# Graph attention on one core: one Q product moved between scores and contexts, split over the array's upper and lower rows

## The chip, the core and the metric

One NeuronCore of a Trainium2 chip runs the whole program. The metric is device time in microseconds (us) from start to end of one execution. Engines run side by side, each through its own queue in order: PE (TensorE, matmuls into PSUM), DVE (VectorE), ACT (ScalarE), POOL (GpSimd) and SP (SyncE, here the queue that issues the DMAs). They meet only at semaphores.

## What is computed

The reference, cut to what matters. `B` is 128 graphs of `S` = 128 nodes, hidden size 384, six heads of 64.

```python
q = heads(x @ Wq + bq);  k = heads(x @ Wk + bk);  v = heads(x @ Wv + bv)
scores = einsum('bhqd,bhkd->bhqk', q, k) / sqrt(64)
probs = softmax(scores + where(adj, 0, -9e15)[:, None], axis=-1)
ctx = einsum('bhqk,bhkd->bhqd', probs, v)          # heads side by side again
out = layernorm(x + ctx @ Wf + bf)                 # over the last axis, eps 1e-5
```

## The kernel before, in words

The 128 graphs go in 32 groups of four (`e` = 0 to 3 names the graph in its group; 512 tokens). Group g is handled by `step`, and parts of three groups share a step. On PE a step is, in this order: the scores of group g (`scores`, L413), three products of Q or K for group g+1 (`qk_product`, L456), the contexts of group g-1 (`ctx_product`, L429), the other three Q or K products of g+1, the output products of g-1 (`out_product`, L449), and the V products of g+1 (`v_product`, L475). All projections (`split_product`, L404 to L411) are made of triples of matmuls of a rounded and a rest part (`hi`, `lo`) in fp32r: nine matmuls for one product, 128 rows by 128 columns of the array, with 512 moving columns for Q and K and 384 for V and output.

Scores and contexts use parts of the array. A head has 64 channels, so a scores matmul reads 64 rows, and two heads go as a couple on the upper and lower 64 rows, into different PSUM banks. A context matmul fills 64 of the array's columns, and two heads go as a couple on the two halves of the columns. In the trace each of these fp32 matmuls is two records, so that a stretch of 24 has 48.

PSUM has eight banks. `scores_ps` is banks 0 to 5: the scores of a group fill all six, the graph e = 0 in banks 0 and 3, e = 1 in 0, 3, 1 and 4, e = 2 in 1, 4, 2 and 5, e = 3 in 2 and 5. The contexts and outputs of g-1 go into banks 0, 3, 1, 4 (`CTX_BANKS`) while group g's scores may still lie there, so `ctx_product` waits on the semaphore `max_found`: two graphs of g must have been read before e = 0 and 1, three before e = 2 and 3 (L440). `work_ps` is the other two banks, which the Q, K and V products use in turn.

DVE reads the scores bank in `mask_and_max` (L626): six passes for a graph (scale, mask, write to `probs`, row maximum), then `neg_max` (L639). The first graph starts when the scores of two are done. ACT exponentiates (`exps`, six activations for a graph), and between them copies the Q and K products out of `work_ps` with the bias (`copy_qk`, L836, semaphore `qk_copied`). DVE inverts the sums (`invert_sums`), POOL multiplies (`normalise_probs`), DVE turns 32x32 blocks (`turn_blocks`), and SP stores and reloads them to finish the transpose (`store_blocks`, `load_blocks`, landing in `pT`), which the contexts of the next step read. ACT rounds the contexts (`round_ctx`), DVE takes the rest (`split_ctx`), PE makes the outputs, DVE adds x and the bias (`add_residual`) and finds mean and variance (`find_stats`), and POOL normalises (`normalise_y`). POOL also adds the bias row to x (`add_bias`, `x_bias`) and turns the adjacency into a mask. The order on every engine is that in which its `step` is written out.

Of the kernel before, what the change touches and what calls it, by code (L numbers as in the profile page):

```python
# [17 lines left out]
ALU = mybir.AluOpType  # L18
ACT = mybir.ActivationFunctionType
# [5 lines left out]
P = 128  # L25
# [5 lines left out]
KC = HID // P  # L31
# [18 lines left out]
TURNS = GROUPS // TURN - 1  # L50

QK_JOBS = [("q", 0), ("k", 0), ("q", 1), ("k", 1), ("k", 2), ("q", 2)]
CTX_BANKS = (0, 3, 1, 4)
NJ = len(QK_JOBS)
HALF = NJ // 2

WARM_UPS = (10, 4)
DMA = 16
# [27 lines left out]
def attention_block(nc, x, adj, wq, bq, wk, bk, wv, bv, wf, bf, out):  # L86
    ctx = ExitStack()
    with ctx:
# [3 lines left out]
        def sem(name):  # L92
            return ctx.enter_context(nc.semaphore(name))
# [70 lines left out]
        def ctx_bank(e):  # L164
            bank = CTX_BANKS[e]
            return scores_ps[:, bank * BANK:(bank + 1) * BANK]

        bias_bank = scores_ps[:, 5 * BANK:5 * BANK + HID]

        def stats_slot(e, n):  # L170
# [78 lines left out]
        exp_done = sem("exp_done")  # L249
        v_copied = sem("v_copied")  # L250
        qk_copied = sem("qk_copied")

        masked_ready = sem("masked_ready")
        x_biased = sem("x_biased")
# [1 line left out]
        rstd_ready = sem("rstd_ready")  # L256
        y_ready = sem("y_ready")
        last_y_ready = sem("last_y_ready")

        def first_of(i, c):  # L260

            return (TURN * i + c) * GROUP
# [140 lines left out]
        def _(pe):  # L403
# [9 lines left out]
            def scores(i, c):  # L413

                g, n = TURN * i + c, first_of(i, c)
                past(pe, qk_copied, g, per=NJ)
# [12 lines left out]
            def ctx_product(i, c, e):  # L429

                g, n = TURN * i + c, first_of(i, c) + e
                past(pe, v_copied, n)
                if isinstance(n, int) and n in TURNED_HERE:
                    pe.wait_ge(pT_copied, 2 * (TURNED_HERE.index(n) + 1))
                else:
                    past(pe, pT_landed[e], g, per=BLOCKS * DMA)
                if isinstance(g, int) and g == LAST:
                    past(pe, y_added, n - GROUP)
                else:
                    past(pe, max_found, first_of(i, c) + GROUP + max(e, 1) - (e == 3))  # L440
# [15 lines left out]
            def qk_product(i, c, j):  # L456

                mat, m = QK_JOBS[j]
                g, n = TURN * i + c, first_of(i, c)
                if isinstance(g, int) and g == 0:  # L460
                    pe.wait_ge(w_split[mat], m + 1)
                past(pe, xT_split, n + GROUP - 1)
                if j < 2:
                    past(pe, v_copied, max(n - GROUP, 0) + 2 + j if isinstance(n, int) else n - GROUP + 2 + j)
                else:
                    past(pe, qk_copied, g * NJ + j - 2)
                split_product(work_ps[j % 2][:, :], lambda k: (
                    w_hi[mat][:, k, m * P:(m + 1) * P], w_lo[mat][:, k, m * P:(m + 1) * P],
                    xT_hi[:, c % TURN, k, :], xT_lo[:, c % TURN, k, :]), qk_done)

            def v_operands(c, e):
                return lambda k: (xT_hi[:, c % TURN, k, tokens(e)], xT_lo[:, c % TURN, k, tokens(e)],
# [2 lines left out]
            def v_product(i, c, e):  # L475


                g, n = TURN * i + c, first_of(i, c) + e
                past(pe, xT_split, n)
                if e >= 2:  # L480
                    past(pe, v_copied, n - 2)
                elif not isinstance(g, int) or g > 0:
                    past(pe, qk_copied, g * NJ + NJ - 2 + e)
                split_product(work_ps[e % 2][:, 0:HID], v_operands(c, e), v_done)

            def first_v():
# [105 lines left out]
        def _(dve):  # L592
# [33 lines left out]
            def mask_and_max(e, n):  # L626
# [5 lines left out]
                for h in range(HEADS):  # L632
# [6 lines left out]
                nc.vector.tensor_scalar(neg_max[:, e, :], row_max[:, e, :], -1.0, None, ALU.mult  # L639
                                        ).then_inc(max_negated, 1)  # L640

            def turn_blocks(i, c, e, n):
# [39 lines left out]
            def step(i, c):  # L682
# [3 lines left out]
                for e in range(3):  # L686
                    mask_and_max(e, n + e)
                invert_sums(0, n)
                mask_and_max(3, n + 3)
                if real(g + 2):  # L690
                    for e in (0, 1):
                        turn_x(i, c + 2, e)
                invert_sums(1, n + 1)
                if real(g + 2):
                    for e in (2, 3):
                        turn_x(i, c + 2, e)
                turn_blocks(i, c, 0, n)
# [3 lines left out]
                turn_blocks(i, c, 1, n + 1)  # L701
                invert_sums(2, n + 2)
# [3 lines left out]
                turn_blocks(i, c, 2, n + 2)  # L706
                if real(g - 1):
                    for e in (0, 1):
                        add_residual(i, c - 1, e, n - GROUP + e)
                    find_stats(0, n - GROUP)  # L710
                invert_sums(3, n + 3)
                if real(g - 1):
                    find_stats(1, n - GROUP + 1)
                    for e in (2, 3):
                        add_residual(i, c - 1, e, n - GROUP + e)
                turn_blocks(i, c, 3, n + 3)
                if real(g + 2):
                    for e in range(GROUP):
                        split_x(c, e, n + 2 * GROUP + e)
                if real(g - 1):  # L720
                    for e in (2, 3):
                        find_stats(e, n - GROUP + e)

            def ending():
                i, c, n = LAST // TURN, LAST % TURN, LAST * GROUP
# [70 lines left out]
        def _(act):  # L796
# [34 lines left out]
            def copy_v(c, e, n):  # L831
                past(act, v_done, n)
                past(act, ctx_done, n - RING)
                nc.scalar.copy(v_sb[:, c % TURN * GROUP + e, :], work_ps[e % 2][:, 0:HID]).then_inc(v_copied, 1)  # L834

            def copy_qk(i, c, j):  # L836

                mat, m = QK_JOBS[j]
# [7 lines left out]
            def step(i, c):  # L846

                g, n = TURN * i + c, first_of(i, c)
                exps(0, n, end=2)
                copy_qk(i, c + 1, 0)  # L850
                exps(0, n, first=2)
                copy_qk(i, c + 1, 1)
                exps(1, n + 1)
# [4 lines left out]
                exps(2, n + 2, end=2)  # L858
                copy_qk(i, c + 1, 3)
                exps(2, n + 2, first=2)  # L860
                copy_qk(i, c + 1, 4)
# [3 lines left out]
                exps(3, n + 3)  # L865
                copy_qk(i, c + 1, 5)
# [183 lines left out]
```

## Time and profile before

| what | value |
|---|---|
| median of 3 runs | 1013.79 us (1013.69 to 1014.57) |
| the profiled execution's own time | 1014.83 us |
| its span in the profile | 1013.0 us |
| PE busy | 1001.5 us, 99% of the span |
| DVE, POOL, ACT busy | 705.5, 629.8, 583.8 us |
| granted PE clock | 0.998 of full speed |
| chain that ended last | PE 95% |

The busy shares say which engine is full; the chain of work that ended last says whether it also sets the end. The steps repeat, so one step in the middle (its scores start at 516.31 us) stands for thirty. T below is the time since the start of a step's scores.

### The profile page before, as it was taken

The numbers are of one execution on the slowest core, as the hardware profiler recorded it, in microseconds if no ns is written. First come the engines' busy times: TensorE is split into PE (matmuls) and PEld (weight loads), VectorE is DVE, ScalarE is ACT, GpSimd is POOL, SyncE is SP. The second block draws the span as 40 slices with busy tenths as digits, with TensorE's granted clock in tenths as the row PEclk, the third lists the DMA queues.
The fourth block names the chain that finished last, engine by engine and source line by source line (L and its number), as shares of the span: only waits on it lengthen the run. The fifth ranks groups of instructions, "written<-read, shape, count | busy, mean of one in ns | idle before, by whom it ended". The sixth has DMA issues, their size and how long they took to land.

```text
span 1013.0 us, 26785 instructions
## 1 busy us (share of the span) xinstructions
PE 1001.5 (99%) x7156; PEld 901.5 (89%) x7156; DVE 705.5 (70%) x2829; ACT 583.8 (58%) x2121; POOL 629.8 (62%) x649
## 2 busy tenths in 40 slices
PE   9999999999999999999999999999999999999996
PEld 8888999888999889998899998899988999988986
DVE  4567766767667677667676676776676766767776
ACT  4665556664556655566645566554666455665552
POOL 2527755567665577555676655775556766557756
PEclk9999999999999999999999999999999999999999
DMA  7366676666766766766667667666676676675443
GB/s 207 81 182 182 185 191 189 174 185 174 197 170 181 187 168 175 195 169 182 181 174 196 168 184 187 163 180 187 171 189 177 176 191 176 181 183 157 150 150 130
DMA packets 339163, 178.06 MB, mean 176 GB/s; under 512 B 222529, under 2 KB 323009, under 8 KB 339137
## 3 DMA queue, kind: packets, MB, share of 16 engines
q1 hardware_dynamic: 337648, 176.77, 63.8%
q10 hardware_dynamic: 1488, 0.98, 0.3%
q8 instruction: 11, 0.18, 0.1%
q14 instruction: 16, 0.12, 0.0%
HBM read 102.96 MB, written 74.71 MB: 175 GB/s over the span
## 4 chain that ended last, share of the span: by engine, by line
PE 95%; ACT 2%; DVE 1%; DMA 1%; issue 0%; DVEq 0%; ACTq 0%
PE work_ps L408 20%; PE work_ps L409 19%; PE work_ps L410 19%; PE scores_ps L444 9%; PE scores_ps L425 9%; PE scores_ps L408 6%; PE scores_ps L409 6%; PE scores_ps L410 6%; ACT probs L825 1%; DMA y_sb<-in_L_gnn_Wq 1%; DVE stats L666 0%; DMA x_in<-in_x 0%; DVE probs L633 0%; ACT qT L843 0%; PE scores_ps L502 0%
## 5 line engine op out<-in xcount | busy, mean ns | idle before, releaser
L979 POOL TENSOR_TENSOR probs<-probs,inv_sum 128x768 f32<-128x768 f32 x128 | 188.5, 1473 | 332.4 <-DVE inv_sum L652 332.4
L825 ACT ACTIVATE probs<-probs,neg_max 128x128 f32<-128x128 f32 x768 | 298.9, 396 | 100.5 <-DVE neg_max L639 100.5
L633 DVE CUSTOM_DVE_ANT_0 probs<-scores_ps,mask_bias 128x128 f32<-128x128 f32 x768 | 172.0, 285 | 83.0 <-PE scores_ps L425 81.9
L974 POOL TENSOR_SCALAR y_sb<-y_sb,mean_var,rstd 128x384 f32<-128x384 f32 x120 | 198.8, 1656 | 21.5 <-POOL rstd L968 21.5
L834 ACT COPY v_sb<-work_ps 128x384 f32<-128x384 f32 x128 | 61.6, 481 | 215.4 <-PE work_ps L410 215.4
L825 ACT ACTIVATION_READ_ACCUMULATOR probs<-probs,neg_max 128x1 f32 x768 | 149.3, 194 | 0.0
L962 POOL TENSOR_TENSOR x_bias<-x_in,bias_row 128x384 f32<-128x384 f32 x128 | 127.6, 1019 | 9.0 <-DVE bias_row L788 9.0
L408 PE MATMUL scores_ps<-wf_hi,cT_hi 128*128 128x384 f32 x384 | 130.1, 339 | 0.0
L409 PE MATMUL scores_ps<-wf_lo,cT_hi 128*128 128x384 f32 x384 | 129.9, 338 | 0.0
L410 PE MATMUL scores_ps<-wf_hi,cT_lo 128*128 128x384 f32 x384 | 129.7, 338 | 0.0
L408 PE MATMUL work_ps<-wv_hi,xT_hi 128*128 128x384 f32 x381 | 128.1, 336 | 0.6 <-ACT qT L843 0.4
L410 PE MATMUL work_ps<-wv_hi,xT_lo 128*128 128x384 f32 x381 | 127.5, 335 | 0.0
L409 PE MATMUL work_ps<-wv_lo,xT_hi 128*128 128x384 f32 x381 | 127.4, 334 | 0.0
L645 DVE STREAM_TRANSPOSE p_turned<-probs 128x768 f32<-128x768 f32 x126 | 120.9, 960 | 5.3 <-DMA p_out<-p_turned 3.7
L408 PE MATMUL work_ps<-xT_hi,wq_hi 128*128 128x512 f32 x288 | 116.1, 403 | 0.1
L408 PE MATMUL work_ps<-xT_hi,wk_hi 128*128 128x512 f32 x288 | 115.8, 402 | 0.0
L409 PE MATMUL work_ps<-xT_lo,wq_hi 128*128 128x512 f32 x288 | 113.0, 392 | 0.0
L409 PE MATMUL work_ps<-xT_lo,wk_hi 128*128 128x512 f32 x288 | 112.5, 391 | 0.0
L410 PE MATMUL work_ps<-xT_hi,wq_lo 128*128 128x512 f32 x288 | 112.4, 390 | 0.0
L410 PE MATMUL work_ps<-xT_hi,wk_lo 128*128 128x512 f32 x288 | 112.1, 389 | 0.0
L843 ACT ACTIVATE kT<-work_ps,bk_col 128x512 f32<-128x512 f32 x96 | 65.2, 679 | 61.1 <-PE work_ps L410 61.1
L660 DVE TENSOR_TENSOR y_sb<-scores_ps,x_bias 128x384 f32<-128x384 f32 x120 | 65.4, 557 | 47.6 <-PE scores_ps L410 47.6
(78 smaller groups left out, 1886.9 us busy)
## 6 DMA issues: line engine op xcount, KB each, us to landing
p_out<-p_turned SPq DMA_DIRECT2D x126, 384.0 KB, 2.8
pT<-p_out SPq DMA_DIRECT2D x504, 96.0 KB, 2.3
x_in<-in_x SPq DMA_DIRECT2D x128, 192.0 KB, 3.0
x_blocks<-in_x SPq DMA_DIRECT2D x360, 64.0 KB, 2.4
out<-y_sb SPq DMA_DIRECT2D x120, 192.0 KB, 2.2
adj_u<-in_adj SPq DMA_DIRECT2D x32, 64.0 KB, 2.1
out<-xT SPq DMA_DIRECT2D x4, 192.0 KB, 1.9
out<-qT SPq DMA_DIRECT2D x4, 192.0 KB, 2.1
```

What stands on the lines that cost most here:

```text
L408: nc.tensor.matmul(dst, s_hi, m_hi, start=k == 0, stop=False)
L409: nc.tensor.matmul(dst, s_hi, m_lo, start=False, stop=False)
L410: last = nc.tensor.matmul(dst, s_lo, m_hi, start=False, stop=k == n_chunks - 1)
L425: last = nc.tensor.matmul(scores_ps[:, score_cols(e, h)], qT[rows, c, h // 2, tokens(e)], kT[rows, c, h // 2, tokens(e)], start=True, stop ...
L444: last = nc.tensor.matmul(dst[half:half + HEAD, h // 2 * SEQ:(h // 2 + 1) * SEQ], v_sb[:, c % TURN * GROUP + e, h * HEAD:(h + 1) * HEAD], ...
L633: last = nc.vector.tensor_tensor_reduce(out=probs[:, e, h, :], in0=scores_ps[:, score_cols(e, h)], in1=mask_bias[:, e, :], scale=SCALE, sc ...
L645: nc.vector.transpose(p_turned[:, e % 2, :, :, :].rearrange("p b h j -> p h b j"), probs[:, e, :, :].rearrange("p h (b k) -> p h b k", b=B ...
L660: nc.vector.tensor_tensor(y_slot(e, n), ctx_bank(e)[:, 0:HID], x_bias[:, c % TURN * GROUP + e, :], ALU.add).then_inc(y_added, 1)
L825: last = nc.scalar.activation(probs[:, e, h, :], probs[:, e, h, :], ACT.Exp, bias=neg_max[:, e, h:h + 1], scale=1.0, accum_out=row_sum[:, ...
L962: nc.gpsimd.tensor_tensor(x_bias[:, slot, :], x_in[:, slot, :], bias_row[:, :], ALU.add).then_inc(x_biased, 1)
L974: nc.gpsimd.tensor_scalar(y_slot(e, n), y_slot(e, n), mean_var[:, at, 0:1], rstd[:, at, 0:1], ALU.subtract, ALU.mult).then_inc(y_ready, 1)
L979: nc.gpsimd.tensor_tensor(probs[:, e, :, :], probs[:, e, :, :], inv_sum[:, e, :].unsqueeze(2).broadcast_to([P, HEADS, SEQ]), ALU.mult).the ...
```

## The change

One product of Q for group g+1, job j = 0, moves from the full array to couples: for each of the three 128-row chunks of the contraction, rows 0 to 63 go to one matmul and rows 64 to 127 to another, into banks 6 and 7 (`qk_halves`). That is 18 matmuls instead of nine, and the same number of columns for each. ACT copies the upper half with the bias (`copy_half`), and DVE adds the lower half to it (`sum_halves`, semaphore `qk_summed`). On PE this product stands alone between scores and contexts, and the five others follow the contexts. Jobs 1 and 2 wait for `qk_summed`. The first group's products are as before.

On DVE the addition stands behind `invert_sums(0)` and ahead of the fourth graph's `mask_and_max`; turning of blocks moves forward and `split_ctx`, `add_residual` and `find_stats` move back. On ACT the exponentials come more in one piece, and the copies of jobs 1 to 5 later. POOL and SP are unchanged.

```diff
+            def qk_halves(i, c, j):
+                mat, m = QK_JOBS[j]
+                n, cols = first_of(i, c), slice(m * P, (m + 1) * P)
+                past(pe, xT_split, n + GROUP - 1)
+                past(pe, v_copied, n - 1)
+                for k in range(KC):
+                    for w, moving in ((w_hi, xT_hi), (w_hi, xT_lo), (w_lo, xT_hi)):
+                        for half in range(2):
+                            rows = slice(half * HEAD, (half + 1) * HEAD)
+                            last = nc.tensor.matmul(half_bank(j, half), w[mat][rows, k, cols],
+                                                    moving[rows, c % TURN, k, :],
...
+                last.then_inc(qk_done, 1)
...
 def step(i, c):                                    (PE)
                 scores(i, c)
-                for j in range(HALF):
-                    qk_product(i, c + 1, j)
+                for j in range(HALVED):
+                    qk_halves(i, c + 1, j)
                 if real(g - 1):
                     for e in range(GROUP):
                         ctx_product(i, c - 1, e)
-                for j in range(HALF, NJ):
+                for j in range(HALVED, NJ):
                     qk_product(i, c + 1, j)
...
+                elif j < HALVED + 2:
+                    pe.wait_ge(qk_summed, HALVED * (g - 1) + 1)
...
+            def sum_halves(i, c, j):
+                dst = (qT if mat == "q" else kT)[:, c % TURN, m, :]
+                dve.wait_ge(half_copied, HALVED * (TURN * i + c - 1) + j + 1)
+                nc.vector.tensor_tensor(dst, half_bank(j, 1), dst, ALU.add).then_inc(qk_summed, 1)
...
+            def copy_half(i, c, j):
+                nc.scalar.activation(dst[:, c % TURN, m, :], half_bank(j, 0), ACT.Identity,
+                                     bias=col[:, m:m + 1], scale=1.0).then_inc(half_copied, 1)
```

PE of the kernel before, in a step, from the end of the scores (`scores_ps<-kT,qT`): the first of three products on the full array.

```order
L425 MATMUL scores_ps<-kT,qT 128x128 x23
L408 MATMUL work_ps<-xT_hi,wq_hi 128x512 [waits v_copied,xT_split]
L409 MATMUL work_ps<-xT_lo,wq_hi 128x512
L410 MATMUL work_ps<-xT_hi,wq_lo 128x512
L408 MATMUL work_ps<-xT_hi,wq_hi 128x512
```

PE of the changed kernel at the same place; L501 is the matmul of `qk_halves`, x2 a couple.

```order
L440 MATMUL scores_ps<-kT,qT 128x128 x23
L501 MATMUL work_ps<-xT_hi,wq_hi 128x512 [waits v_copied,xT_split]
L501 MATMUL work_ps<-xT_hi,wq_hi 128x512
L501 MATMUL work_ps<-xT_lo,wq_hi 128x512 x2
L501 MATMUL work_ps<-xT_hi,wq_lo 128x512 x2
L501 MATMUL work_ps<-xT_hi,wq_hi 128x512 x2
```

Before, 27 such matmuls stand between the scores and the contexts; now 18, as nine couples, and the contexts come right behind them.

DVE of the kernel before, in a step, from the last `neg_max` on: transposes of x, the block transposes `p_turned` and the rests of the contexts `cT_lo`.

```order
L639 TENSOR_SCALAR neg_max<-row_max 128x6 [waits max_found]
L617 STREAM_TRANSPOSE xT<-x_blocks 128x384 [waits xT_split,x_blocks_loaded1] x2
L652 RECIPROCAL inv_sum<-row_sum 128x6 [waits probs_ready,exp_done]
L617 STREAM_TRANSPOSE xT<-x_blocks 128x384 [waits xT_split,x_blocks_loaded1] x2
L645 STREAM_TRANSPOSE p_turned<-probs 128x6x4x32 [waits p_stored0,probs_ready]
L609 TENSOR_TENSOR cT_lo<-scores_ps,cT_hi 128x384 [waits cT_hi_ready] x2
L645 STREAM_TRANSPOSE p_turned<-probs 128x6x4x32 [waits p_stored1,probs_ready]
L652 RECIPROCAL inv_sum<-row_sum 128x6 [waits probs_ready,exp_done]
L609 TENSOR_TENSOR cT_lo<-scores_ps,cT_hi 128x384 [waits cT_hi_ready] x2
```

DVE of the changed kernel at the same place.

```order
L675 TENSOR_SCALAR neg_max<-row_max 128x6 [waits max_found]
L695 RECIPROCAL inv_sum<-row_sum 128x6 [waits probs_ready,exp_done]
L653 STREAM_TRANSPOSE xT<-x_blocks 128x384 [waits xT_split,x_blocks_loaded1] x2
L688 STREAM_TRANSPOSE p_turned<-probs 128x6x4x32 [waits p_stored0,probs_ready]
L695 RECIPROCAL inv_sum<-row_sum 128x6 [waits probs_ready,exp_done]
L653 STREAM_TRANSPOSE xT<-x_blocks 128x384 [waits xT_split,x_blocks_loaded1] x2
L688 STREAM_TRANSPOSE p_turned<-probs 128x6x4x32 [waits p_stored1,probs_ready]
L695 RECIPROCAL inv_sum<-row_sum 128x6 [waits probs_ready,exp_done]
L645 TENSOR_TENSOR cT_lo<-scores_ps,cT_hi 128x384 [waits cT_hi_ready] x2
```

All four sums are now inverted ahead of the first rest of a context.

## Rows read from the trace of the kernel before

**Rows 1.** The page, part 4: the chain that ended last, by engine.

```profile
PE 95%; ACT 2%; DVE 1%; DMA 1%; issue 0%; DVEq 0%; ACTq 0%
```

**Rows 2.** Stretches of one step: window, length; busy PE, PEld, DVE, ACT, POOL.

```profile
516.31:519.19 2.88, 2.88 (x50) 2.76 (x49) 0.94 (x9) 0.48 (x1) 2.71 (x3) 1.00 0.73 221
519.19:525.57 6.38, 6.38 (x29) 4.98 (x27) 5.71 (x45) 4.77 (x21) 5.09 (x5) 1.00 0.81 212
525.57:528.34 2.77, 2.77 (x49) 2.60 (x48) 2.70 (x7) 2.77 (x12) 2.77 (x5) 1.00 0.13 47
528.34:534.60 6.26, 6.26 (x29) 5.18 (x28) 3.15 (x7) 4.43 (x19) 2.17 (x4) 1.00 0.70 169
...
sum 30.97, PE 30.97 PEld 27.95 DVE 21.89 ACT 18.09 POOL 19.83; mean PE 5.16 PEld 4.66 DVE 3.65 ACT 3.01 POOL 3.31
```

**Rows 3.** Timeline of PE in that step: start, length, operation; the changes of shape.

```profile
516.31 2.95 PE L425 MATMUL scores_ps<-kT,qT 64*128 64x128 f32 x48
...
519.19 0.50 PE L408 MATMUL work_ps<-xT_hi,wq_hi 128*128 128x512 f32 x1
519.53 0.40 PE L409 MATMUL work_ps<-xT_lo,wq_hi 128*128 128x512 f32 x1
...
525.25 0.39 PE L410 MATMUL work_ps<-xT_hi,wq_lo 128*128 128x512 f32 x1
525.57 2.84 PE L444 MATMUL scores_ps<-pT,v_sb 128*64 128x128 f32 x48
528.34 0.50 PE L408 MATMUL work_ps<-xT_hi,wk_hi 128*128 128x512 f32 x1
528.68 0.40 PE L409 MATMUL work_ps<-xT_lo,wk_hi 128*128 128x512 f32 x1
```

**Rows 4.** Timeline of PE, a narrow window: the last three couples of the scores.

```profile
518.75 0.50 PE L425 MATMUL scores_ps<-kT,qT 64*128 64x128 f32 x6
```

**Rows 5.** Timeline of DVE, same step: first pass and negation of three graphs.

```profile
518.25 0.29 DVE L633 CUSTOM_DVE_ANT_0 probs<-scores_ps,mask_bias 128x128 f32<-128x128 f32 x1 [2.73 <-PE scores_ps L425]
...
519.64 0.36 DVE L639 TENSOR_SCALAR neg_max<-row_max 128x6 f32<-128x6 f32 x1
520.00 0.29 DVE L633 CUSTOM_DVE_ANT_0 probs<-scores_ps,mask_bias 128x128 f32<-128x128 f32 x1
...
521.39 0.58 DVE L639 TENSOR_SCALAR neg_max<-row_max 128x6 f32<-128x6 f32 x1
521.88 0.28 DVE L633 CUSTOM_DVE_ANT_0 probs<-scores_ps,mask_bias 128x128 f32<-128x128 f32 x1
...
523.26 0.17 DVE L639 TENSOR_SCALAR neg_max<-row_max 128x6 f32<-128x6 f32 x1
```

**Rows 6.** Timeline of POOL beside them.

```profile
518.32 1.65 POOL L974 TENSOR_SCALAR y_sb<-y_sb,mean_var,rstd 128x384 f32<-128x384 f32 x1 [0.18 <-POOL rstd L968]
519.94 2.98 POOL L962 TENSOR_TENSOR x_bias<-x_in,bias_row 128x384 f32<-128x384 f32 x3
```

**Rows 7.** Timelines of PE and DVE, second step, POOL idle: scores' start, third negation.

```profile
50.91 0.38 PE L425 MATMUL scores_ps<-kT,qT 64*128 64x128 f32 x2
...
57.31 0.17 DVE L639 TENSOR_SCALAR neg_max<-row_max 128x6 f32<-128x6 f32 x1
```

**Rows 8.** Groups by shape: count, busy us and mean ns, idle before.

```profile
L825 ACT ACTIVATE probs<-probs,neg_max 128x128 f32<-128x128 f32 x768 | 298.9, 396 | 100.5 <-DVE neg_max L639 100.5
L843 ACT ACTIVATE qT<-work_ps,bq_col 128x512 f32<-128x512 f32 x96 | 65.5, 683 | 26.8 <-PE work_ps L410 26.8
L660 DVE TENSOR_TENSOR y_sb<-scores_ps,x_bias 128x384 f32<-128x384 f32 x120 | 65.4, 557 | 47.6 <-PE scores_ps L410 47.6
L617 DVE STREAM_TRANSPOSE xT<-x_blocks 128x384 f32<-128x384 f32 x120 | 62.0, 555 | 0.7
```

**Rows 9.** Timeline of PE, second step: the contexts and what follows.

```profile
62.91 0.88 PE L444 MATMUL scores_ps<-pT,v_sb 128*64 128x128 f32 x12 [0.55 <-issue]
63.72 0.50 PE L408 MATMUL work_ps<-xT_hi,wk_hi 128*128 128x512 f32 x1
```

More of the change, by code:

```diff
@@ L52 @@
 QK_JOBS = [("q", 0), ("k", 0), ("q", 1), ("k", 1), ("k", 2), ("q", 2)]
+HALVED = 1
+HALF_BANKS = ((6, 7),)
 CTX_BANKS = (0, 3, 1, 4)
 NJ = len(QK_JOBS)
-HALF = NJ // 2
 WARM_UPS = (10, 4)
@@ L166, in ctx_bank, with half_bank @@
             return scores_ps[:, bank * BANK:(bank + 1) * BANK]
+        def half_bank(j, half):
+            bank = HALF_BANKS[j][half]
+            return work_ps[bank - 6][:, :] if bank >= 6 else scores_ps[:, bank * BANK:(bank + 1) * BANK]
         bias_bank = scores_ps[:, 5 * BANK:5 * BANK + HID]
@@ L251, in attention_block @@
         qk_copied = sem("qk_copied")
+        half_copied = sem("half_copied")
+        qk_summed = sem("qk_summed")
         masked_ready = sem("masked_ready")
@@ L258, in attention_block, with copies @@
         last_y_ready = sem("last_y_ready")
+        def copies(g, j):
+            return (NJ - HALVED) * g + j + 1
         def first_of(i, c):
@@ L415, in scores @@
                 g, n = TURN * i + c, first_of(i, c)
-                past(pe, qk_copied, g, per=NJ)
+                pe.wait_ge(qk_copied, copies(g, NJ - 1))
+                if not isinstance(g, int) or g > 0:
+                    pe.wait_ge(qk_summed, HALVED * g)
                 past(pe, y_added, n - GROUP - 1)
@@ L439, in ctx_product @@
                 else:
-                    past(pe, max_found, first_of(i, c) + GROUP + max(e, 1) - (e == 3))
+                    past(pe, max_found, first_of(i, c) + GROUP + (1 if e < 2 else 2))
                 dst = ctx_bank(e)
@@ L462, in qk_product @@
                 past(pe, xT_split, n + GROUP - 1)
-                if j < 2:
-                    past(pe, v_copied, max(n - GROUP, 0) + 2 + j if isinstance(n, int) else n - GROUP + 2 + j)
+                if isinstance(g, int) and g == 0:
+                    if j < 2:
+                        pe.wait_ge(v_copied, GROUP - 1 + j)
+                    else:
+                        pe.wait_ge(qk_copied, copies(0, j - 2))
+                elif j < HALVED + 2:
+                    pe.wait_ge(qk_summed, HALVED * (g - 1) + 1)
                 else:
-                    past(pe, qk_copied, g * NJ + j - 2)
+                    pe.wait_ge(qk_copied, copies(g, j - 2))
                 split_product(work_ps[j % 2][:, :], lambda k: (
@@ L469, in qk_product @@
                     xT_hi[:, c % TURN, k, :], xT_lo[:, c % TURN, k, :]), qk_done)
+            def qk_halves(i, c, j):
[9 more added lines that the diff above has]
+                                                    moving[rows, c % TURN, k, :],
+                                                    start=k == 0 and w is w_hi and moving is xT_hi,
+                                                    stop=k == KC - 1 and w is w_lo)
+                last.then_inc(qk_done, 1)
             def v_operands(c, e):
@@ L482, in v_product @@
                 elif not isinstance(g, int) or g > 0:
-                    past(pe, qk_copied, g * NJ + NJ - 2 + e)
+                    pe.wait_ge(qk_copied, copies(g, NJ - 2 + e))
                 split_product(work_ps[e % 2][:, 0:HID], v_operands(c, e), v_done)
@@ L688, in step @@
                 invert_sums(0, n)
+                sum_halves(i, c + 1, 0)
                 mask_and_max(3, n + 3)
+                invert_sums(1, n + 1)
                 if real(g + 2):
@@ L692, in step @@
                         turn_x(i, c + 2, e)
-                invert_sums(1, n + 1)
+                turn_blocks(i, c, 0, n)
+                invert_sums(2, n + 2)
                 if real(g + 2):
@@ L696, in step @@
                         turn_x(i, c + 2, e)
-                turn_blocks(i, c, 0, n)
+                turn_blocks(i, c, 1, n + 1)
+                invert_sums(3, n + 3)
                 if real(g - 1):
@@ L700, in step @@
                         split_ctx(e, n - GROUP + e)
-                turn_blocks(i, c, 1, n + 1)
-                invert_sums(2, n + 2)
+                turn_blocks(i, c, 2, n + 2)
+                turn_blocks(i, c, 3, n + 3)
                 if real(g - 1):
@@ L705, in step @@
                         split_ctx(e, n - GROUP + e)
-                turn_blocks(i, c, 2, n + 2)
-                if real(g - 1):
[L708 to L722, printed above, removed]
+                for e in range(GROUP):
+                    if real(g + 2):
+                        split_x(c, e, n + 2 * GROUP + e)
+                    if real(g - 1) and e > 0:
+                        add_residual(i, c - 1, e - 1, n - GROUP + e - 1)
+                        find_stats(e - 1, n - GROUP + e - 1)
+                if real(g - 1):
+                    add_residual(i, c - 1, 3, n - GROUP + 3)
+                    find_stats(3, n - GROUP + 3)
             def ending():
@@ L834, in copy_v @@
                 nc.scalar.copy(v_sb[:, c % TURN * GROUP + e, :], work_ps[e % 2][:, 0:HID]).then_inc(v_copied, 1)
+            def copy_half(i, c, j):
+                mat, m = QK_JOBS[j]
+                g = TURN * i + c
+                past(act, qk_done, g * NJ + j)
+                past(act, scores_done, (g - 2) * GROUP + GROUP - 1)
+                dst, col = (qT, bq_col) if mat == "q" else (kT, bk_col)
+                nc.scalar.activation(dst[:, c % TURN, m, :], half_bank(j, 0), ACT.Identity,
+                                     bias=col[:, m:m + 1], scale=1.0).then_inc(half_copied, 1)
             def copy_qk(i, c, j):
@@ L848, in step @@
                 g, n = TURN * i + c, first_of(i, c)
-                exps(0, n, end=2)
-                copy_qk(i, c + 1, 0)
-                exps(0, n, first=2)
+                exps(0, n)
+                copy_half(i, c + 1, 0)
+                exps(1, n + 1)
+                exps(2, n + 2, end=4)
                 copy_qk(i, c + 1, 1)
-                exps(1, n + 1)
+                exps(2, n + 2, first=4)
                 copy_qk(i, c + 1, 2)
@@ L857, in step @@
                         round_ctx(e, n - GROUP + e)
-                exps(2, n + 2, end=2)
+                exps(3, n + 3, end=3)
                 copy_qk(i, c + 1, 3)
-                exps(2, n + 2, first=2)
-                copy_qk(i, c + 1, 4)
+                exps(3, n + 3, first=3)
                 if real(g - 1):
@@ L864, in step @@
                         round_ctx(e, n - GROUP + e)
-                exps(3, n + 3)
-                copy_qk(i, c + 1, 5)
+                for j in (4, 5):
+                    copy_qk(i, c + 1, j)
                 if real(g + 2):
```

1 line of the change is left out of this document (added).

## The prediction

> **What bounds the kernel now.** I read the chain that ended last first, since a busy share alone does not say who sets the end: PE is 95% of it [rows 1]. Then one step cut into its stretches [rows 2]: scores 2.88 us, three products 6.38, contexts 2.77, three products 6.26, and the rest of the 30.97, 12.68, for outputs and V. PE is busy in all of them and waits for nobody; the step repeats with the same length, so the middle one stands for thirty. So what counts is PE's own time between matmuls, and whether a new order makes it wait. Then the timeline of PE at the places where the shape changes [rows 3, 4], and at last DVE and POOL just behind the scores [rows 5, 6], because the change brings the contexts near to them.
>
> **What the change removes.** A product's matmuls follow each other at 0.228 us ((534.60 - 528.68) over 26, by the end of the stretch in rows 2 and the second row after the contexts in rows 3). Where the shape changes it takes longer. The last three scores couples start at 518.75 and need 0.11 us each, so they are through at 519.09, yet the full array starts at 519.19: 0.10 us to leave. Its first matmul holds 0.34 us instead of 0.23: 0.11 us to enter [rows 3, 4]. From the full array into the contexts it is 0.32 instead of 0.228 (525.25 to 525.57), 0.09, and some 0.05 for their first couple. Before, a step goes full, rows, full, columns, full; now full, rows, columns, full. One leaving and one entering go, 0.10 + 0.11 = 0.21 us. The three products behind the scores also take 6.38 where 27 times 0.228 and their entry and exit give 6.36; with that 0.02 the gain is 0.23 us a step. The Trainium skill has the rule for it (TensorEngine Tiling (Array Packing), Key Properties): a change of tiling mode drains the engine, a change of tile alone does not. The trace agrees, with the 0.10 us above, and rows to columns is also a change of mode, so the page too gives one drain less, not two.
>
> **What the couples cost.** No row shows fp32r couples with 512 columns. From above, no overlap at all: 18 times 0.228 = 4.10 us. From below, couples as dense as 512 columns at the granted 2.4 GHz: 9 times 0.213 = 1.92. The nearest row is the scores: 48 records on half the rows in 2.88 us, 0.12 for a couple of 0.27 us long records, so that two halves do run together [rows 3]. I take 9 times 0.228 = 2.05. Their two weight loads fit: the scores hide two in 0.11 us.
>
> **What now waits.** The contexts. Times are T, from the start of the scores. Scores end at T+2.78 without leaving their mode, couples at T+4.83, contexts could start at T+4.93 with the 0.10 for the change. Before they started at T+9.26 (525.57), long after DVE was through. Context 0 and 1 need the maxima of two graphs, 2 and 3 of three. DVE starts its first graph at T+1.94 (518.25), since it waits for the scores of two; the second negation, right behind the second maximum, starts at T+5.08 (521.39), the third at T+6.95 (523.26) [rows 5]. PE wants the third at 4.93 + 0.05 + 1.31 = T+6.29 (half of the contexts' 2.77 less 0.15 is 1.31). So PE stands still, and the stretch ends when DVE says so: whatever the couples gain up to there is lost. The first wait, T+4.93 to T+5.08, is inside the second.
>
> How late is the third maximum then? In the rows the first negation takes 0.36 us and ends at 520.00 with POOL's instruction (518.32 + 1.65 = 519.97), the second 0.58 and ends at 521.97 near the end of the second of three `x_bias` additions (519.94 + 2 x 0.99 = 521.92), the third, with less beside it, 0.17 [rows 5, 6]. Where POOL does nothing, the third negation starts at 57.31 - 50.91 = T+6.40 [rows 7]; inside the loop DVE begins 0.15 later, which makes T+6.55. POOL's work is unchanged but its place in the step follows DVE's statistics, which the change moves. So the bounds are T+6.55 and T+6.95, and I take the middle, T+6.75, as one collision is likely to stay. The Trainium skill (SBUF — State Buffer, Who interferes with whom) says why a small operation can take so long: GpSimd and VectorE share a port pair, and the later one is blocked until the other's whole instruction ends. Rows 5 and 6 agree, to 0.05 us; by that rule each negation waits for at most one POOL instruction.
>
> **The sum for a step.** Contexts 2 and 3 from T+6.75: 0.05 + 1.31 + 0.10 = 1.46, to T+8.21. Five products: 6.26 + 18 x 0.228 = 10.36. Outputs and V 12.68. Together 31.25, against 30.97: +0.28 us. With T+6.55 it is +0.08, with T+6.95 +0.48. Had PE not to wait, it would be 4.93 + 2.77 + 10.36 + 12.68 = 30.74, -0.23.
>
> **What else moves, at nothing if the cover holds.** Jobs 1 and 2 wait for `qk_summed`. ACT starts exponentials at about T+3.7, six take 2.3, and the half's copy then 0.68, to T+6.7 [rows 8]. DVE inverts the sums at T+6.9 and adds from T+7.15 for 0.557 x 512/384, about 0.7 [rows 8]: T+7.85, 0.36 before PE wants job 1. Behind that waiting addition is the fourth graph's maximum, which nobody on PE needs until the next scores. This is what would be late next if the contexts did not wait. ACT's 24 exponentials (0.39 each), copies and casts end near T+17.2, as they wait a little for jobs 1 and 2; DVE then gives the first `cT_lo` at about T+17.8, and outputs start at T+18.6. The blocks that the contexts read are turned some 5 us sooner than before, which covers that the contexts themselves come 4.3 us sooner. SP and POOL have no new operation. Additions and maximum together keep DVE at 22.6 us of 31.
>
> **The first two steps.** In step 0 PE waits for the sum, from T+4.8 to T+7.9, part of which comes back later. It does not matter: in step 1 the last context waits for its blocks, which come by DMA, and starts at 62.91 [rows 9], after a chain that begins on DVE and SP, not on PE. Behind these contexts stood 6.26 us of products and now 10.36: +4.1 us, once. The chain can begin up to two x transposes sooner (2 x 0.555 us, rows 8), so +3.0 to +4.1; I take 3.5. The steps 2 to 30 are 29, and the ending is unchanged.
>
> **Result.** 3.5 + 29 x 0.28 = +11.6 us (bounds 3.0 + 2.3 = 5.3 and 4.1 + 13.9 = 18.0). On the profiled execution, 1014.83, that is 1026.4; it stood 1.0 above the median of the runs, 1013.79, so the time to expect is **1025.4**, from 1019.1 to 1031.8.
>
> **Rivals.** (1) The couples do not overlap in fp32r. Nothing in the profile shows that they do; the scores speak against it. Then they end at T+6.9, DVE is nearly through, the step is 30.74 + 2.05 = 32.79, +1.82: 4 + 29 x 1.82 = +56.8, 1070.6. In between, DVE's wait hides couples of up to 0.228 + (6.75 - 6.29)/9 = 0.28 us. Chance 0.10. (2) Faster: the contexts do not wait, because DVE has the third maximum by T+6.29. It decides there: 0.11 us before the fastest row. Then -0.23 a step, or -0.36 if couples also take 0.213: 3.5 - 6.7 or 3.5 - 10.4, 1010.6 or 1006.9. The three graphs' passes at T+6.40 speak against it. The Trainium skill (TensorE: Matmul & The Clock Gate, Part 3) puts row-packed matmuls at one duration plus about 4 ns a tile, so the page gives near 0.217 for a couple, inside this rival's second price. Chance 0.10. (3) Between: DVE is never held by POOL and starts as early as in the second step, T+6.40: -0.07 a step, 1015.3. Chance 0.07. (4) A further wait (sum, copies of jobs 2 or 3, `cT_lo` of the first context) adds up to 0.4 us a step: 1037. Chance 0.05. The forecast itself has 0.68.
>
> A measurement of this kernel tells about 0.2%, 2 us, from no change. Faster 0.10 (rival 2), same 0.08 (rival 3 and the edge), slower 0.82. The range that holds 8 in 10 takes in the forecast with its bounds, rivals 3 and 4 and the near end of 2, and leaves out rival 1 and the far end of 2: 1010 to 1038.
>
> **What would show it.** In the changed profile: nine couples in 2.05 us behind the scores; PE idle before context 2, released by DVE's row maximum, until about T+6.75; the third negation there; DVE's addition done before T+8.2; a step of 31.25. I am wrong if the couples take 4 us, if PE waits nowhere there, or if another wait on PE is longer than that one.

## The result: slower by 1.6%, and the profile after

The changed kernel takes 1030.85 us (median of 4 runs, 1030.04 to 1032.31) beside 1013.76 for the kernel before: a ratio of 1.0164, 95% interval 1.0152 to 1.0176, or +17.1 us. The forecast was slower, +11.6 us with bounds of 5.3 and 18.0.

The chain that ended last, the line that answers to [rows 1]:

```profile
PE 82%; DVE 13%; issue 3%; DMA 1%; DVEq 1%; ACT 0%
```

PE no longer sets the end alone: an eighth of the chain now runs over DVE. One step, cut at the same places as in [rows 2] (window, length, busy time of PE, PEld, DVE, ACT, POOL, then the granted PE clock as a share of full speed, the DMA share and GB/s): scores, the couples with what follows them, contexts, five products, outputs, V.

```profile
558.72:561.42 2.70, 2.70 (x49) 2.70 (x50) 0.76 (x7) 0.48 (x1) 2.52 (x3) 1.00 0.76 168
561.42:563.87 2.45, 2.33 (x24) 1.59 (x20) 2.38 (x20) 1.27 (x7) 2.10 (x3) 1.00 0.81 226
563.87:567.09 3.22, 3.00 (x49) 2.58 (x49) 2.99 (x23) 3.22 (x16) 1.14 (x1) 1.00 0.72 229
567.09:577.44 10.35, 10.35 (x47) 8.55 (x46) 6.40 (x19) 9.46 (x37) 6.60 (x9) 1.00 0.59 149
...
sum 31.40, PE 31.06 PEld 27.85 DVE 22.13 ACT 18.19 POOL 19.86; mean PE 5.18 PEld 4.64 DVE 3.69 ACT 3.03 POOL 3.31
```

The contexts took 2.77 us and now take 3.22, and the stretch of the couples is 0.2 us longer than the couples are. PE's timeline of the same step answers to [rows 3]:

```profile
558.72 2.95 PE L440 MATMUL scores_ps<-kT,qT 64*128 64x128 f32 x48
561.42 0.48 PE L501 MATMUL work_ps<-xT_hi,wq_hi 64*128 64x512 f32 x2
561.74 0.39 PE L501 MATMUL work_ps<-xT_lo,wq_hi 64*128 64x512 f32 x2
...
563.36 0.40 PE L501 MATMUL work_ps<-xT_hi,wq_lo 64*128 64x512 f32 x2
563.87 1.53 PE L459 MATMUL scores_ps<-pT,v_sb 128*64 128x128 f32 x24
565.62 1.53 PE L459 MATMUL scores_ps<-pT,v_sb 128*64 128x128 f32 x24 [0.22 <-DVE row_max L669]
```

Nine couples follow each other at 0.23 us ((563.36 - 561.74) / 7), so the two halves run together, also in fp32r. Then PE waits twice for a row maximum, ahead of the first context and ahead of the third. DVE and POOL, the answer to [rows 5, 6]:

```profile
560.66 0.29 DVE L669 CUSTOM_DVE_ANT_0 probs<-scores_ps,mask_bias 128x128 f32<-128x128 f32 x1 [3.98 <-PE scores_ps L440]
...
562.05 0.51 DVE L675 TENSOR_SCALAR neg_max<-row_max 128x6 f32<-128x6 f32 x1
...
563.85 0.17 DVE L675 TENSOR_SCALAR neg_max<-row_max 128x6 f32<-128x6 f32 x1
564.21 0.29 DVE L669 CUSTOM_DVE_ANT_0 probs<-scores_ps,mask_bias 128x128 f32<-128x128 f32 x1 [0.19 <-issue]
...
565.61 0.17 DVE L675 TENSOR_SCALAR neg_max<-row_max 128x6 f32<-128x6 f32 x1
...
565.79 0.65 DVE L683 TENSOR_TENSOR qT<-work_ps,qT 128x512 f32<-128x512 f32 x1
```
```profile
560.56 2.96 POOL L1011 TENSOR_TENSOR x_bias<-x_in,bias_row 128x384 f32<-128x384 f32 x3
```

The second and third negation start at 563.85 and 565.61, and PE goes on at 563.87 and 565.62, right behind each. The third stands at T+6.89. The last row is the addition of the halves.

Over the whole execution, the scores of the third and of the thirty-first step start at

```profile
87.64 0.60 PE L440 MATMUL scores_ps<-kT,qT 64*128 64x128 f32 x6
...
967.74 0.49 PE L440 MATMUL scores_ps<-kT,qT 64*128 64x128 f32 x4
```

which makes a mean step of (967.74 - 87.64) / 28 = 31.43 us. In the kernel before it is (949.93 - 82.68) / 28 = 30.97. So 28 steps bring +12.9 us. The first two steps together went from 54.55 to 58.40 us, +3.9. The remaining 0.7 of the span's 17.5 us has three parts: the first scores start 1.1 us later (29.23 against 28.14; in the profiles of all these kernels they start between 27.7 and 29.2), the thirty-first step is 0.4 us longer (26.67 against 26.29), and the last one with the ending 0.7 us shorter.

### The profile page after: what moved, and what is told of

Read it like the earlier page. It is cut to its first block, busy times and chain, and to the rows that moved or that the text cites. A ratio compares the mean times of both kernels' runs of the same rounds, so it can differ in the third digit from the quotient of the medians.

```text
span 1030.5 us, 27417 instructions
## 1 busy us (share of the span) xinstructions
PE 1004.1 (97%) x7435; PEld 899.7 (87%) x7435; DVE 716.9 (70%) x2860; ACT 587.0 (57%) x2121; POOL 630.3 (61%) x649
## 4 chain that ended last, share of the span: by engine, by line
PE 82%; DVE 13%; issue 3%; DMA 1%; DVEq 1%; ACT 0%
PE work_ps L421 18%; PE work_ps L423 17%; PE work_ps L422 17%; DVE probs L669 11%; PE scores_ps L421 7%; PE scores_ps L422 7%; PE scores_ps L423 7%; PE scores_ps L459 5%; PE scores_ps L440 5%; DMA y_sb<-in_L_gnn_Wq 1%; DVEq L72 1%; DVE row_max L669 1%; DVE neg_max L675 0%; DMA x_in<-in_x 0%; PE scores_ps L538 0%
## 5 line engine op out<-in xcount | busy, mean ns | idle before, releaser
L1017 POOL TENSOR_TENSOR rstd<-var_eps,minus_half 128x1 f32<-128x1 f32 x128 | 80.0, 627 | 140.3 <-DVE var_eps L716 140.3
L688 DVE STREAM_TRANSPOSE p_turned<-probs 128x768 f32<-128x768 f32 x126 | 117.4, 947 | 3.4 <-DMA p_out<-p_turned 3.3
L459 PEld LDWEIGHTS scores_ps<-pT,v_sb 128*64 128x64 f32 x1536 | 82.7, 137 | 36.3 <-DVE row_max L669 29.5
L459 PE MATMUL scores_ps<-pT,v_sb 128*64 128x128 f32 x1536 | 98.2, 277 | 15.1 <-DVE row_max L669 8.4
L695 DVE RECIPROCAL inv_sum<-row_sum 128x6 f32<-128x6 f32 x128 | 24.4, 191 | 124.2 <-ACT probs L864 124.0
L440 PEld LDWEIGHTS scores_ps<-kT,qT 64*128 64x128 f32 x1536 | 88.2, 188 | 8.5 <-issue 7.7
```

The source lines that it names most:

```text
L1017: nc.gpsimd.tensor_tensor(rstd[:, at, :], var_eps[:, at, :], minus_half[:, :], ALU.pow).then_inc(rstd_ready, 1)
```

## The experiments

The theory A is the forecast's: a step loses what PE waits for the third graph's row maximum, and the new shape and order are otherwise what they cost before, less one change of shape. The main rival B: couples, or contexts right behind them, cost PE the time. What each kernel showed, in one table; T is as before, the third negation is where the third graph's maximum is ready (mean, or range where the steps differ), the contexts' stretch runs from their first matmul to the next product (so a wait ahead of the first is not in it), the step is the mean from the third step to the thirty-first, and ratios are to the kernel before on the same chip.

| kernel | us | ratio (95%) | third negation, T+ | contexts' stretch | mean step |
|---|---|---|---|---|---|
| before | 1013.8 | 1 | 6.95 | 2.77 | 30.97 |
| changed | 1030.85 | 1.0164 (1.0152 to 1.0176) | 6.88 | 3.22 | 31.43 |
| e1 before, two passes | 1013.43 | 0.9991 (0.9982 to 1.0001) | 5.88 | 2.77 | 30.97 |
| e2 changed, two passes | 1015.26 | 1.0010 (0.9998 to 1.0023) | 6.05 to 6.78 | 2.77 to 3.30 | 30.93 |
| e3 as e2, no couples | 1016.35 | 1.0026 (1.0015 to 1.0036) | 6.05 to 6.67 | 2.77 to 2.98 | 31.00 |
| e4 changed, no couples | 1030.61 | 1.0164 (1.0147 to 1.0181) | 6.87 to 7.04 | 3.19 | 31.41 |
| e5 changed, POOL moved | 1026.67 | 1.0112 (1.0095 to 1.0129) | 6.83 | 3.21 | 31.35 |
| e8 changed, waits ahead | 1029.26 | 1.0147 (1.0116 to 1.0177) | 6.72 to 7.16 | 2.97 | 31.42 |
| e10 changed, both | 1014.55 | 1.0003 (0.9994 to 1.0013) | 6.38 | 2.90 | 30.89 |
| e9 two passes, POOL moved | 1010.74 | 0.9956 (0.9939 to 0.9973) | 5.88 | 2.77 | 30.76 |
| e7 as e9, waits ahead, second step | 1011.12 | 0.9963 (0.9949 to 0.9977) | 5.43 | 2.77 | 30.76 |
| e11 as e9, no couples | 1017.31 | 1.0019 (1.0008 to 1.0031) | 5.88 | 2.77 | 30.99 |
| e6 two products ahead | 1015.79 | 1.0014 (1.0005 to 1.0024) | 6.83 to 7.41 | 2.77 | 30.97 |

**Is it the wait?** e1 and e2 make DVE's passes fewer and longer, in the kernel before and in the changed one. Three heads share a maximum, which softmax allows; the negation and the bias of the exponentials, not shown, follow it.

```diff
-                for h in range(HEADS):
-                    last = nc.vector.tensor_tensor_reduce(
-                        out=probs[:, e, h, :], in0=scores_ps[:, score_cols(e, h)], in1=mask_bias[:, e, :],
+                for r in range(2):
+                    first = r * MATS * BANK + e * HID
+                    last = nc.vector.tensor_tensor_reduce(
+                        out=probs[:, e, r::2, :],
+                        in0=scores_ps[:, first:first + HID].rearrange("p (j k) -> p j k", k=SEQ),
+                        in1=mask_bias[:, e, :].unsqueeze(1).broadcast_to([P, MATS, SEQ]),
...
```

> The kernel before with fewer, longer passes of VectorE over the scores: two for a graph (three heads each, one maximum shared by the three) instead of six (one for a head). Nothing else is changed. The control for the runs with the same edit. Every theory: PE does not wait there in the kernel before, the contexts start at T+9.3 and the third maximum was there at T+6.9, so the time stays at 1013.8 us within 0.2%, while the third negation moves from T+6.95 to about T+6.0.

> The changed kernel with two passes for a graph instead of six. Theory A (the contexts of the changed kernel wait for the third maximum, and that is what a step loses): the third negation comes near T+5.95, ahead of the T+6.3 at which PE wants it, the wait is gone, the step is 30.74 us instead of 31.40 and the whole 29 x 0.66 = 19 us shorter, about 1012 us: a little faster than the kernel before. Rival B (the couples, or contexts right behind them, cost PE the time itself): the row maximum's wait goes but the step stays above 31.2, about 1028 us.

e1 is the same as before: the third negation came a full microsecond sooner and nobody had waited for it. The same edit took 15 us off the changed kernel, so rival B falls. But e2 missed its 1012: the mean step was 30.93, from 30.75 to 31.30, and only 11 of the 28 were 30.77 or less. PE's timeline of e2 in one of these, and the second and third negation in this step and the next:

```profile
549.74 2.95 PE L440 MATMUL scores_ps<-kT,qT 64*128 64x128 f32 x48
554.71 2.87 PE L459 MATMUL scores_ps<-pT,v_sb 128*64 128x128 f32 x48
```
```profile
554.59 0.17 DVE L678 TENSOR_SCALAR neg_max<-row_max 128x2 f32<-128x2 f32 x1
...
556.02 0.17 DVE L678 TENSOR_SCALAR neg_max<-row_max 128x2 f32<-128x2 f32 x1
...
584.96 0.92 DVE L678 TENSOR_SCALAR neg_max<-row_max 128x2 f32<-128x2 f32 x1
...
586.86 0.17 DVE L678 TENSOR_SCALAR neg_max<-row_max 128x2 f32<-128x2 f32 x1
```
```profile
583.86 1.99 POOL L1014 TENSOR_TENSOR x_bias<-x_in,bias_row 128x384 f32<-128x384 f32 x2
```

The negation at 584.96 lasts until 585.88, and POOL's additions end at 583.86 + 1.99 = 585.85. With shorter passes the negations fall elsewhere on POOL's work, and a long one can take back most of what the passes gave.

e9 adds to e2 a move on POOL alone; POOL's own work stays the same.

```diff
-                for e in range(3):
-                    add_bias(i, c, e, n + e)
                 normalise_probs(0, n)
                 for e in (0, 1):
                     make_mask_bias(i, c + 1, e)
-                add_bias(i, c, 3, n + 3)
                 normalise_probs(1, n + 1)
                 for e in (2, 3):
                     make_mask_bias(i, c + 1, e)
+                for e in range(GROUP):
+                    add_bias(i, c, e, n + e)
```

> Two passes for a graph and GpSimd's bias additions moved as above, couples kept. In the run with two passes alone the negations of most steps were held by GpSimd for up to 0.98 us and the contexts still waited in most steps (third negation T+6.05 to T+6.8); the steps that did not wait were 30.76. Expected: third negation near T+5.95 in every step, no wait ahead of the contexts, every step 30.74 to 30.76, so 28 x 0.19 = 5 us less than with two passes alone, 1010 us, 0.4% faster than the kernel before. If what holds the contexts is not GpSimd: the steps stay at 30.93 on average and the time near 1015 us.

Every step is 30.76, every negation 0.17 us, and the contexts start at T+4.96 and run through:

```profile
547.95 2.95 PE L440 MATMUL scores_ps<-kT,qT 64*128 64x128 f32 x48
552.91 2.84 PE L459 MATMUL scores_ps<-pT,v_sb 128*64 128x128 f32 x48
```

1010.74 us, 0.44% under the kernel before, and with e7 (1011.12) the fastest kernel of this study. So the change does what it is for once nothing waits, and theory A holds with its size: 31.43 to 30.76, 0.67 us a step, is the wait.

**What are couples worth?** e4, e3 and e11 take the couples out and keep the order: an ordinary product stands between scores and contexts (`qk_product` in place of `qk_halves`, ACT's `copy_qk` in place of `copy_half`, no addition on DVE), with six passes, two passes, and two passes with POOL moved.

```diff
-                for j in range(HALVED):
-                    qk_halves(i, c + 1, j)
+                for j in range(BETWEEN):
+                    qk_product(i, c + 1, j)
```

> The changed order with six passes as in the changed kernel, but an ordinary product in place of the couples (nine matmuls on all rows, no addition by VectorE). Theory A: the contexts end when VectorE lets them, so what stands ahead of them matters little: within 0.1 us a step of the changed kernel, 1028 to 1033 us, with the third negation at T+6.9 again. Rival B: without couples the loss is gone and the time is near the kernel before, 1014 to 1018 us.

> The changed order with two passes for a graph, but the product that stands alone between scores and contexts is an ordinary one: nine matmuls on all 128 rows, one copy by ScalarE, no addition by VectorE. Set beside the run with couples it gives the price of one change of array shape with no wait in the way. If leaving and entering cost what the trace of before shows (0.10 + 0.11 us, and 0.02 of slower matmuls): 0.2 us a step, 31 steps, 6 us slower than with couples, about 1018 us. If couples bring nothing by themselves: equal to the run with couples.

> Two passes for a graph, GpSimd's additions moved, and an ordinary product in place of the couples: the twin of the run at 1010.7 us without couples, with no wait ahead of the contexts in either. Its step should be 30.98 against 30.76, 0.22 us for one leaving and one entering of the full array, 28 x 0.22 = 6.2 us: 1017 us.

Where DVE holds the contexts, couples or not is all one: e4 is the changed kernel to 0.2 us. Where nothing holds them, e11 beside e9 prices them: 30.99 against 30.76, 0.23 us a step, and 1017.31 against 1010.74. The step is the better measure: e11's ten executions spread from 1014.6 to 1019.7. e3 came out 2 us under its number and shows why a twin without a wait was needed: the ratio of e3 to e2 is small because e2's longer waits hide part of it.

e6 puts two ordinary products ahead of the contexts (BETWEEN = 2), with six passes:

> The changed order with six passes and no couples, but two ordinary products between scores and contexts and four behind, where the kernel before has three and three. PE reaches the contexts at T+7.3, after the third maximum at T+6.9. Theory A: no wait, a step of 30.97 as in the kernel before, and only what the first two steps cost on top (one product more behind the contexts of the second step, 2.05 us): 1016 us. If the order on the other engines is what costs: 1020 us or more.

It is 30.97 in every step, as the kernel before. PE comes to the contexts at T+7.22 and to the third at T+8.59, and the latest third negation is at T+7.41, so nothing waits. The rest of the changed order on DVE and ACT costs nothing in a step. The cost in the first two steps is 0.9 us (55.45 against 54.55), not the 2 expected.

**How late is the maximum, and why?** This is the term that the forecast sized wrong. e5 moves POOL's additions only, as in e9; e8 moves DVE's waits; e10 does both.

```diff
-                past(dve, masked_ready, n)
-                past(dve, blocks_turned, n - GROUP)
+                if isinstance(n, int) or e == 0:
+                    late = n if isinstance(n, int) else n + GROUP - 1
+                    past(dve, masked_ready, late)
+                    past(dve, blocks_turned, late - GROUP)
```

> The changed kernel with GpSimd's four bias additions moved behind the second multiplication of the probabilities, so that GpSimd has next to nothing to do while VectorE passes over the first three graphs. The negations should all take 0.17 us. Theory C, as in the prediction (GpSimd's instructions alone make the third maximum late, and without them the third negation stands at T+6.55 as worked out from the second step): step 31.08 instead of 31.41, 28 steps, about 9 us less than the changed kernel, 1021 us. Rival S (the queue of VectorE needs 0.36 us from a negation to the next graph's first pass inside the loop whatever GpSimd does, as the second and third graph of the changed kernel show): the first graph's gap shrinks from 0.42 to 0.36 only, third negation at T+6.83, step 31.35, 2 us less, 1029 us.

> The changed kernel where, inside the loop, VectorE waits for the masks and the earlier block transposes of all four graphs at once ahead of the first graph, instead of graph by graph, so that only the wait for the scores stands ahead of the others. GpSimd is as in the changed kernel. Rival S (waits against computed values on VectorE's queue cost the time between graphs): the gap from the second negation to the third graph's first pass goes from 0.36 towards 0.22, the third negation to about T+6.75, the step is about 0.1 us shorter, 3 to 4 us in all, 1026 us. Theory C: no change, 1030 us.

> The changed kernel (six passes, couples) with both edits: GpSimd's additions moved away, and VectorE's waits for masks and transposes ahead of the first graph. With GpSimd moved alone the third negation went from T+6.88 to T+6.83 only, and with the waits ahead alone the third gap shrank from 0.36 to 0.12 to 0.22 but GpSimd held the first negation for 0.65 to 1.09 us. If the two terms add as read (gaps of 0.22 and nobody holding): passes from T+1.88, third negation T+6.47 to T+6.55, contexts' wait 0.2 us, step 31.0 to 31.05 instead of 31.35, so 28 x 0.3 = 9 us less than with GpSimd moved alone: 1018 us. If the gap of 0.36 has another cause: 1026 us.

DVE of e5, where POOL does nothing beside it:

```profile
563.05 0.17 DVE L675 TENSOR_SCALAR neg_max<-row_max 128x6 f32<-128x6 f32 x1
563.41 0.29 DVE L669 CUSTOM_DVE_ANT_0 probs<-scores_ps,mask_bias 128x128 f32<-128x128 f32 x1 [0.19 <-issue]
...
564.80 0.17 DVE L675 TENSOR_SCALAR neg_max<-row_max 128x6 f32<-128x6 f32 x1
```

DVE of e10 at the same place:

```profile
553.02 0.17 DVE L677 TENSOR_SCALAR neg_max<-row_max 128x6 f32<-128x6 f32 x1
553.14 0.29 DVE L671 CUSTOM_DVE_ANT_0 probs<-scores_ps,mask_bias 128x128 f32<-128x128 f32 x1
...
554.53 0.17 DVE L677 TENSOR_SCALAR neg_max<-row_max 128x6 f32<-128x6 f32 x1
```

From a negation to the next graph's first pass it is 0.36 us in e5, of which 0.19 is idle with nothing in the profile that ends it ("issue"). In e10, where these two waits stand ahead of the first graph alone, it is 0.21 behind the first negation and 0.12 behind the second. So the gap of 0.36 is a floor that is there without POOL, and POOL's hold of the first negation had stood almost wholly inside it: e5 moved the third negation by 0.05 us only, as rival S said. Its time, 1026.67, lies between rival S's 1029 and theory C's 1021; the mean step, 31.35, is rival S's. e8 alone did next to nothing either, since POOL then held the first negation for longer:

```profile
559.70 0.90 DVE L677 TENSOR_SCALAR neg_max<-row_max 128x6 f32<-128x6 f32 x1
...
561.89 0.17 DVE L677 TENSOR_SCALAR neg_max<-row_max 128x6 f32<-128x6 f32 x1
...
563.40 0.17 DVE L677 TENSOR_SCALAR neg_max<-row_max 128x6 f32<-128x6 f32 x1
```

Together they move it by half a microsecond, to T+6.38, the step goes to 30.89 and the time to 1014.55 (1018 expected, with gaps of 0.22). Each of two covers hid the other: 4 us for one, 1.6 for the other, 16 for both, or by 28 mean steps 2.4, 0.4 and 15.1. The edit shows that the gap comes from these two waits as they stand in the loop. In the steps written out the same waits, for constants, leave 0.22 (second step of the changed kernel); whether in the loop it is the waiting or the working out of the awaited value is not shown, and what the queue does in the 0.19 us the trace does not tell.

**The second step.** e7 is e9 with DVE's waits ahead and, in the second step alone, jobs 1 and 2 ahead of the contexts.

```diff
+                early = HALVED + 2 if isinstance(g, int) and g == 1 else HALVED
...
+                for j in range(HALVED, early):
+                    qk_product(i, c + 1, j)
```

> As the kernel before this one in the list (two passes, GpSimd moved), with VectorE's waits for masks and transposes ahead of the first graph, and in the second step alone the products of jobs 1 and 2 ahead of the contexts. The second step's contexts wait for blocks that come by DMA at about 62.9 us whatever PE does; two products put in that wait should give back 3 to 4 us, once. Expected 1006 to 1008 us, 0.7% faster than the kernel before. If the blocks' landing is not what holds the second step: no gain over the other, 1010 us.

A miss: 1011.12, no better than e9. In the second step job 1 itself waits for the sum, to T+6.94, so that the contexts end 2.73 us later than in e9 (13.97 instead of 11.24 from the start of the scores) with 4.1 us of products done: 1.4 us gained. But the first step was 1.6 us longer than in e9. Two stretches show why, 3.5 and 3.4 us long, the first from the start of the last couple; e7 first, then e9:

```profile
32.37:35.90 3.53, 1.60 (x9) 1.05 (x6) 2.83 (x12) 3.53 (x18) 2.00 (x3) 1.00 0.01 2
35.90:39.32 3.42, 3.42 (x9) 2.63 (x8) 1.98 (x4) 3.23 (x15) 2.88 (x4) 0.50 0.09 35
```
```profile
33.21:36.73 3.52, 1.59 (x9) 1.05 (x6) 2.83 (x12) 3.52 (x18) 2.00 (x3) 1.00 0.01 2
36.73:40.15 3.42, 3.42 (x16) 2.81 (x15) 2.23 (x6) 3.35 (x16) 2.87 (x4) 1.00 0.09 35
```

In e7 PE was granted half its clock, 1.2 instead of 2.4 GHz, for these 3.42 us. Nine of its matmuls fall into them and 16 of e9's into the same time: they follow each other at 0.43 us instead of 0.23, and the seven that are missing take 1.6 us later on. Just before, PE had stood still for 1.9 us, waiting for the sum. The first steps of e2, e8 and e10 have the same fall, 3.4 us long, at the same wait (2.3 to 2.4 us); the changed kernel, e5 and e9 have the wait there and no fall. In e5 and e11 it comes in the second step, at the wait for the blocks (2.4 and 2.3 us). In all six it begins between 0.3 us before the end of the wait and 1.2 us after it. So the time is explained, but what decides whether the clock falls at such a wait is open. None of these falls lies in the 28 steps of the mean. Without it e7 would stand near 1009.5 (an estimate, 1011.1 - 1.6), still short of 1008: the gain in the second step was 1.4 us, not 3 to 4.

## Right, and where the sum was short

The mechanism was right step by step. PE set the end and a step repeats [rows 1, 2]. The couples overlap: 0.23 us each against the 0.228 taken, which settles rival 1 (1070.6) by the profile alone. One leaving and one entering go: 0.23 us forecast, 0.23 measured by e11 and e9. The contexts would start at T+4.93 and do so at T+4.96 in e9, and an unhindered step of 30.74 is 30.76. In the changed kernel PE goes on within 0.02 us of the third negation. DVE's addition is done at T+7.7 (565.79 + 0.65), ahead of PE at T+8.4. Rival 2, no wait, needs the third maximum by T+6.3: its condition was right, as e9 shows with T+5.88, and the changed kernel is not there. Rival 3, T+6.40 without POOL, is ruled out by e5, T+6.83. Rival 4 is not seen in the steps.

The spans of the two profiled executions differ by 17.5 us, 5.9 more than the forecast's 11.6, and the largest part is one term: **the third negation, T+6.75 forecast, T+6.88 measured**. Its lower bound, T+6.55, was worked out from the second step [rows 7], which is written out and not in the loop, with one correction, 0.15 us, for the loop's later first pass. In the loop the same lateness comes again ahead of the second and third graph, 0.14 us each (0.36 instead of 0.22). Without POOL it is therefore T+6.83 (e5), so the bounds lay from T+6.83 to T+6.95 and the middle of the two could not be T+6.75. The rows of before did not show this floor, because the two longer negations there were held by POOL for as long or longer [rows 5, 6]. So the prediction put down to POOL what in the changed kernel is mostly DVE's own queue: POOL adds 0.05 us to T+6.83. That the upper bound, T+6.95, covered the measured value although it was taken from a step in which POOL held both negations is in part luck.

The terms of the 5.9: 28 steps of 31.39 instead of 31.25 make 3.9 us; steps in which POOL held the first negation for 0.6 to 0.95 us, up to 31.8 long, make 1.1 (0.04 in the mean); the first two steps 0.4 (3.9 instead of 3.5); the thirty-first step 0.1 (0.38 instead of 0.28); the later first scores 1.1, and the shorter ending takes 0.7 back. Whether the last two come from the change is not shown.

The second step's last context; the second row answers to [rows 9]:

```profile
58.27 2.42 PE L459 MATMUL scores_ps<-pT,v_sb 128*64 128x128 f32 x36
63.81 0.88 PE L459 MATMUL scores_ps<-pT,v_sb 128*64 128x128 f32 x12 [3.11 <-issue]
```

It waits there as foreseen, for 3.1 us. It starts at 63.81 where 62.91 or sooner was forecast, but the first scores of this execution were 1.1 us later too. Counted from them it is 34.6 us, against 34.8 before: 0.2 sooner of the 0 to 1.1 allowed for, which with 4.1 us of products behind it makes the 3.9.

## What to carry to other kernels

Moving work closer to what produced its buffers trades a small sure gain (0.23 us for a change of array shape) for a wait that was not there before: read when the releasing engine is through, not how busy it is. Where an engine has two reasons to be late, take both away before saying that neither matters: here 4 us and 1.6 us alone, 16 together. And a bound taken from steps written out in full does not hold in the loop; take it from a step of the loop. And where the same matmuls take longer in one execution, read the granted clock of that stretch first.

## What was not expected of the hardware

- A wait on DVE's queue inside the loop costs time if nothing covers it: 0.36 us from the start of a 0.17 us negation to the next pass, with 0.19 us idle ("issue"), and 0.12 to 0.21 without two of those waits (e10).
- A TENSOR_SCALAR of 6 elements a row takes 0.17 us or up to 1.09 us, until POOL's running instruction ends. The Trainium skill (SBUF — State Buffer, Who interferes with whom) describes this lock, and the traces agree (585.88 against 585.85; of 558 negations longer than 0.21 us in the thirteen traces, 557 end within 0.06 us of the end of a POOL instruction). New here is that it depends on the phase of the two engines, so that any edit that shifts either can bring it or take it away.
- fp32r matmuls on 64 rows with 512 columns run as couples at 0.23 us, as a single matmul on 128 rows does.
- PE's granted clock fell to half for 3.4 us in six of the thirteen executions, each time at a wait of PE of 1.9 us or more in the first two steps. In e7 against e9 it cost 1.6 us. Other executions had waits as long and no fall.
